# Spreading C over eight heads by DMA instead of by a TensorE product, with the plan of step times made anew

## The chip, the cores and the metric

The kernel runs on one core of a Trainium2 chip. The metric is the device time of one execution in microseconds (us); lower is better. A core has TensorE (PE, matrix products), VectorE (DVE), ScalarE (ACT), GpSimd (POOL) and SyncE (SP, whose queue issues every DMA of this kernel). Each engine runs its own list of instructions in order and waits on semaphores for the others.

## The reference

One layer: x = x + ssm(layernorm(x)), then x = x + ffn(layernorm(x)), on x of 8 x 1024 x 256 in float32. The change lies in the state space part, here cut to what it touches:

```python
z0, x0 = zxbcdt[..., :512], zxbcdt[..., 512:1024]
xBC = silu(causal_conv4(zxbcdt[..., 1536:2080]) + conv_b)
dt = softplus(zxbcdt[..., -8:] + dt_bias)
A = -exp(A_log)                       # 8 heads of 64 channels
x, Bm, Cm = xBC[..., :512], xBC[..., 512:528], xBC[..., 528:544]
def step(h, inp):                     # state h: heads x 64 x 16
    x_t, B_t, C_t, dt_t = inp
    h = exp(dt_t * A) * h + dt_t * x_t * B_t
    return h, einsum('bhpn,bn->bhp', h, C_t) + D_param * x_t
# then layernorm(y), y * sigmoid(y @ W_gate.T), concat with silu(z0) * x0, @ W_out.T
# ffn: gelu(x @ ternary(W_fc).T), layernorm, @ ternary(W_proj)
```

All eight heads share the same 16 rows of C. The part of y that comes from the state carried in is, for each head, the state times C scaled by that head's decay up to the time step; so C is wanted on 8 x 16 = 128 rows, once for each head.

## The kernel before

The 8 x 1024 time steps are cut into 16 blocks of 512 (two a sequence), and each block into four chunks of 128. For every block 16 tasks are made (`ln1, conv, silu, dt_chain, inputs, decay, states, mix, yout, gate, skip, out, turn3, ln3, fc, proj`), each a Python generator that yields a `Need` (an engine, what must be ready, how many PSUM banks, which table of ScalarE's functions) ahead of each step.

The order on the engines is written out at build time by a list scheduler: it keeps the tasks of up to five blocks alive, works out for each when its next step could start by the costs in `Engine.guess` and `Engine.dma`, and of the steps that could start within `EPS` = 0.4 of the earliest it takes the one whose due time is least. The due time is the step's number in `PLAN`, plus `PERIOD` (76.4) times the block, plus the block's entry in `SHIFT`. A step that wants another function table starts later by `SWITCH`. So `PLAN` settles ties between steps that can start together; it holds no step back. A DMA counts as 0.5 on SP there. What comes out is five fixed lists of instructions.

The places that the change touches:

- `silu(i)`: once channel group 4 of the convolution is done (`conv4`), ScalarE writes silu of B into `xbuf[64:80, 4]` and silu of C into `cv[64:80, i % 2, 4]` (token `ct`), 16 rows of 512 each; then it runs over the 512 x channels in two instructions.
- `decay(i)`: TensorE sums the log decays (`pick` with `segL`), ScalarE's Exp writes `ec` (128 x 512: head and state row by time). Then `rep` (16 x 128, ones where the state rows agree) times C gives C on all 128 rows in a PSUM bank (token `rep_mm`), and VectorE multiplies it into `ec` (token `ce`), after copying the chunk ends to `dec`. Then come the scaled B (`BE`) and the product of B and C (`Gm`).
- `states(i)` needs `dec` and `ce`; `yout(i)` multiplies the states with `ec` and adds the products within the chunk, then normalises y.
- The users of SP's queue: `hilo_T`, which splits a matrix into two float16 halves in `hb` and has both transposed by DMA (`xnT` for a block's input, `x3T` ahead of `fc`, `hT` for each of the four chunks of `fc`, ahead of `proj`'s products on the same chunk); `load_x`; the residual's load in `out`; `dt_chain`'s four copies `segR<-segL`; and the output.

The weights are float16 pairs, and a product of two pairs is three matmuls (`three`, the profile's line 166). Products of float32 tiles, `rep`'s among them, are run as they are.

Of the kernel before, what the change touches and what calls it, by code (L numbers as in the profile page):

```python
# [8 lines left out]
P = 128  # L9
T = 512  # L10
# [9 lines left out]
for _n, _w in (("dtb", 1), ("alog", 8), ("dcol", 4), ("lng", 4), ("lnb", 4), ("bg", 4), ("cw", 20), ("cb", 5),  # L20
# [8 lines left out]
PLAN = {  # L29
    "conv": (-101.6, -85.2, -84.1, -81.5, -77.0, -79.4, -67.1, -67.5, -66.0, -61.0, -57.8, -59.7, -55.3, -49.8,  # L30
        -46.5, -45.2, -44.4, -42.1),
    "decay": (-4.9, -4.9, 0.3, 8.1, 8.6, 9.2, 12.6, 17.1, 17.2, 10.0, 19.8),
    "dt_chain": (-66.4, -63.6, -38.0, -33.7, -26.6, -21.4, -21.3, -18.8, -18.1, -17.2),
# [4 lines left out]
    "gate": (108.4, 112.0, 122.6, 122.9, 120.0, 117.1, 125.3, 125.7, 125.1, 130.0, 131.7, 130.6, 130.8, 135.1,  # L38
        136.7, 135.8),
    "inputs": (-21.6, -5.6, 0.7, 1.1, 1.6, 4.8, 2.1, 7.1),  # L40
    "ln1": (-111.6, -95.8, -93.5, -92.7, -93.9, -92.0),
    "ln3": (198.2, 200.0),
    "mix": (4.7, 9.5, 27.4, 29.3, 20.0, 32.8, 27.1, 33.6, 33.9, 37.3, 41.0, 47.1),
    "out": (106.3, 145.0, 162.2, 168.2, 184.7, 197.2, 194.4, 191.4, 195.3),
    "proj": (227.6, 230.4, 229.2, 239.6, 238.3, 242.4, 249.7, 254.7),
    "silu": (-32.6, -33.5, -33.7),
    "skip": (50.6, 53.1, 52.7, 56.2, 117.3, 117.3, 117.8, 115.9, 121.7, 122.1, 120.3, 121.4, 118.2, 99.2,
        100.5, 101.8, 103.4, 128.5, 127.9, 127.2),
    "states": (20.0, 24.7, 26.0),
    "turn3": (195.1, 195.6, 193.9, 199.7),  # L50
    "wffn": (88.0, 97.1, 101.0, 103.0, 108.9, 103.0, 113.3, 113.1, 116.3, 115.9, 118.0),
    "wgate": (70.5,),
    "win": (12.4, 16.7, 23.0),
    "wout": (88.8, 89.0),
    "yout": (29.7, 29.6, 47.0, 75.6, 76.1, 75.3, 74.2, 63.8, 65.9, 65.6, 67.1, 68.6, 70.4, 74.1, 74.8, 82.6,
        84.1, 85.8, 89.1, 89.0, 90.4, 93.6, 94.6, 97.4, 91.5, 101.1, 101.6, 103.5, 102.6, 100.1, 105.7, 102.2,
        104.7, 105.7),
}
PERIOD = 76.4
SHIFT = (0.0, 0.0, 0.0, 0.0, 0.0, 0.0, 0.0, 0.0, 0.0, 0.0, 0.0, 0.0, 0.0, -0.4, 0.0, 2.4)  # L60
AHEAD = 5
EPS = 0.4

# [132 lines left out]
def build(nc, x_d, small_d, const_d, c16_d, lnw_d, win_d, wg_d, wout_d, wfc_d, wpj_d, out_d):  # L196
# [5 lines left out]
    with ctx:  # L202
        def sb(name, shape, dt=f32):
            return ctx.enter_context(nc.sbuf_tensor(name, shape, dt))

        def sem(name):
            return ctx.enter_context(nc.semaphore(name))
# [13 lines left out]

        small = sb("small", [P, NSMALL])
        const = sb("const", [P, 3 * P + 2])
        ident, smask, rep = const[:, 0:P], const[:, P:2 * P], const[64:80, 2 * P:3 * P]
        ul = sb("ul", [P, 2, P], f16)
        upto, after = ul[:, 0, :], ul[:, 1, :]
        ones16 = sb("ones16", [P, P], f16)[:, :]
# [435 lines left out]
        def decay(i):  # L663
            cs, ct, bb = cv[:, i % 2], cv[64:80, i % 2, 4, :], xbuf[64:80, 4, 3:T + 3]
            yield Need(V, ("car", i - 1), ("S", 4 * i) if i % 2 else ("car", i - 1))
            if i % 2 == 0:
                dn["S", 4 * i] = V.do([old("car", i - 1)], "memset", S[:, (4 * i) % 5, :], 0.0)
            yield Need(PE, ("L", i), ("car", i - 1), banks=1, func="Exp")
            b, f = take()
            PE.wait(dn["L", i], f, dn["tk", 0])  # L670
            for c in range(NCH):
                m = PE.do([], "matmul", b[:, chunk(c)], pick[:, c, :, :], segL[:, i % 2, :], start=True, stop=True)
            dn["ec_mm", i] = m
            yield Need(A, ("ec_mm", i), func="Exp")
            dn["ec", i] = A.do([m, old("car", i - 1)], "activation", ec[:, :], b[:, :], ACT.Exp)
            give(b, dn["ec", i])
            yield Need(PE, ("a", i), ("be", i - 1), banks=1, func="Exp")
            b, f = take()
            PE.wait(f, t_ul)
            for q in range(2):  # L680
                m = PE.do([dn["a", i]], "matmul", b[:, 0:32].rearrange("p (c e) -> p c e", c=NCH), after,
                          ahl[:, i % 2, q, :, 3:11], start=(q == 0), stop=(q == 1))
            dn["ahl_read", i] = m
            yield Need(A, ("ahl_read", i), func="Exp")
            dn["es", i] = A.do([m, old("be", i - 1)], "activation", esuf[:, :, :].rearrange("p c e -> p (c e)"),
                               b[:, 0:32], ACT.Exp)
            give(b, dn["es", i])
            yield Need(PE, ("ct", i), ("S_done", i - 1), banks=1)
            b, f = take()
            m = PE.do([dn["ct", i], f, tc], "matmul", b[:, :], rep, ct, start=True, stop=True)  # L690
            dn["rep_mm", i] = m
            yield Need(V, ("rep_mm", i), ("ec", i))
            v = V.do([dn["ec", i], old("S_done", i - 1)], "tensor_copy", dec[:, :],
                     ec[:, :].rearrange("p (c t) -> p c t", c=NCH)[:, :, P - 1])
            dn["ce", i] = V.do([m, v], "tensor_tensor", ec[:, :], b[:, :], ec[:, :], ALU.mult)
            give(b, dn["ce", i])
            yield Need(PE, ("es", i), ("S_done", i - 1), ("L", i), banks=1)
            b, f = take()
            PE.wait(f)
            for c in range(NCH):  # L700
                m = PE.do([dn["ct", i]], "transpose", b[:, 16 * c:16 * c + 16], bb[:, chunk(c)], ident[64:80, 64:80])
            dn["be_mm", i] = m
            yield Need(V, ("be_mm", i))
            dn["be", i] = V.do([m, dn["es", i], old("S_done", i - 1), dn["L", i]], "tensor_tensor", BE[:, :, :, :],
                               b[:, 0:64].rearrange("p (c n) -> p c n", c=NCH).unsqueeze(2).broadcast_to([P, NCH, 8, 16]),
                               esuf[:, :, :].unsqueeze(3).broadcast_to([P, NCH, 8, 16]), ALU.mult)
            give(b, dn["be", i])
            yield Need(PE, ("ct", i), ("EM_all", i - 1), banks=1)
            b, f = take()
            PE.wait(f)  # L710
# [406 lines left out]
```

How the kernel before makes its waits and increments, by code:

```python
    def wait(self, *tokens):  # L87
        for t in tokens:
            if t is None:
                continue
            if isinstance(t, list):
                self.wait(*t)
                continue
            sem, value = t
            self.due = max(self.due, t.when)
            if self.met.get(id(sem), 0) >= value:
                continue
            self.met[id(sem)] = value
            self.queue.append(lambda e, sem=sem, value=value: e.wait_ge(sem, value))
# [33 lines left out]
    def do(self, waits, name, *args, **kw):  # L133
        self.wait(*waits)
        if self.kind == "ACT":
            self.load(args[2].name)
        self.count += 1
        sem = self.sem
        method = {
            "matmul": lambda e: e.matmul(*args, **kw), "transpose": lambda e: e.transpose(*args, **kw),
            "activation": lambda e: e.activation(*args, **kw),
            "tensor_tensor": lambda e: e.tensor_tensor(*args, **kw),
            "tensor_scalar": lambda e: e.tensor_scalar(*args, **kw),
            "scalar_tensor_tensor": lambda e: e.scalar_tensor_tensor(*args, **kw),
            "tensor_copy": lambda e: e.tensor_copy(*args, **kw), "memset": lambda e: e.memset(*args, **kw),
            "bn_stats": lambda e: e.bn_stats(*args, **kw), "bn_aggr": lambda e: e.bn_aggr(*args, **kw),
        }[name]
        self.queue.append(lambda e: method(e).then_inc(sem, 1))
        return Token(sem, self.count, self.spend(name, args, kw))
```

## Time and profile before

| what | value |
|---|---|
| median of 3 runs | 1315.84 us (1315.33 to 2367.39) |
| time of the profiled execution | 1316.03 us |
| its span | 1314.2 us |
| instructions | 22448 |
| PE busy | 1169.8 us, 89% |
| PE loading weights (PEld, overlaps PE) | 740.1 us, 56% |
| DVE busy | 1070.4 us, 81% |
| ACT busy | 937.2 us, 71% |
| POOL busy | 363.7 us, 28% |

The span runs from the first to the last instruction; the 1.8 us beyond it are start and end. The rows in the section further down are of this one execution. Of the three runs two lie within 0.51 us of each other, and the third is an outlier. L140, L141, L142, L144 and so on are the lines of `Engine.do` that issue matmul, activation, tensor_tensor and scalar_tensor_tensor; L178 and L180 are the transposing and the plain DMA; so instructions are told apart by their tiles.

### The profile page before, as it was taken

To read this page: it belongs to the slowest core of one execution; us is meant where nothing else is said; L and a number is where in the kernel's file an instruction comes from. 1 tells how busy PE (TensorE), PEld (TensorE's weight loads), DVE (VectorE), ACT (ScalarE), POOL (GpSimd) and SP (SyncE) were. 2 spreads that over 40 slices of the span, in tenths; PEclk is the share of its full clock that TensorE was granted. 3 is DMA by queue.
4 is the path that set the end of the run, shared out by engine and by line. 5 is a ranking of instruction groups with operands and counts; after the bars stand their busy time and mean duration, and the time that the engine had idled before them with its cause. 6 is when DMAs were issued, how large, how long until landed. Compare 5 with 4: busy or idle time off the path is not lost.

```text
span 1314.2 us, 22448 instructions
## 1 busy us (share of the span) xinstructions
PE 1169.8 (89%) x8566; PEld 740.1 (56%) x8566; DVE 1070.4 (81%) x2116; ACT 937.2 (71%) x1502; POOL 363.7 (28%) x388
## 2 busy tenths in 40 slices
PE   3566889999999999999999998999899999999875
PEld 1344465656566565656566564656656565746453
DVE  6878798888988988888989896888888887766534
ACT  5746377878789696767878776777868686665734
POOL 0010315142422415142330514142050424232320
PEclk9777899999999999999999999999999999999987
DMA  4610102222242323223232313223232231312433
GB/s 142 201 33 1 33 1 63 51 71 61 64 82 65 65 55 74 44 57 82 65 66 65 66 33 89 57 65 80 51 66 58 56 65 49 66 49 49 97 64 80
DMA packets 234874, 84.89 MB, mean 65 GB/s; under 512 B 205712, under 2 KB 233104, under 8 KB 234768
## 3 DMA queue, kind: packets, MB, share of 16 engines
q1 hardware_dynamic: 234768, 83.47, 28.8%
q8 instruction: 68, 1.11, 0.4%
q14 instruction: 38, 0.31, 0.1%
HBM read 24.32 MB, written 8.39 MB: 25 GB/s over the span
## 4 chain that ended last, share of the span: by engine, by line
PE 43%; DVE 28%; ACT 14%; DMA 10%; issue 4%; POOL 1%; DVEq 0%; SPq 0%
PE bank L140 23%; PE bank L166 20%; DMA hT<-hb 8%; DVE hn L144 4%; DVE cv L144 4%; ACT h L141 3%; DVE EM L144 3%; ACT L161 3%; DVE hb L142 3%; DVE tg L144 2%; ACT hb L141 2%; DVE sz L144 2%; DVE S L144 1%; DVE yhl L142 1%; DVE x L143 1%
## 5 line engine op out<-in xcount | busy, mean ns | idle before, releaser
L166 PE MATMUL bank<-xnT,win 128*128 128x512 f16 (+1 forms) x1040 | 267.9, 390 | 17.0 <-DMA xnT<-hb 16.8
L144 DVE SCALAR_TENSOR_TENSOR cv<-xbuf,cws,cv 128x512 f32<-128x512 f32 (+1 forms) x240 | 179.5, 749 | 12.6 <-ACT cv L141 4.8
L140 PE MATMUL bank<-wpj,hT 128*128 128x256 f16 x1040 | 136.3, 289 | 47.9 <-DMA hT<-hb 42.0
L166 PEld LDWEIGHTS bank<-xnT,win 128*128 128x128 f16 (+1 forms) x1040 | 102.2, 102 | 130.1 <-issue 32.7
L166 PE MATMUL bank<-yhl,wg 128*128 128x512 f16 x704 | 165.3, 384 | 3.7 <-DVE yhl L142 3.6
L140 PEld LDWEIGHTS bank<-wpj,hT 128*128 128x128 f16 x1040 | 103.7, 103 | 80.8 <-ACT hb L141 16.7
L161 ACT ACT_TABLE_LOAD x97 | 124.5, 1283 | 15.8 <-DVE dtt L144 7.1
L140 PE MATMUL bank<-wfc,x3T 128*128 128x512 f16 x512 | 128.5, 385 | 4.3 <-DMA x3T<-hb 4.3
L142 POOL TENSOR_TENSOR rsy<-rsy,mhalf 128x1 f32<-128x1 f32 x64 | 59.4, 928 | 241.2 <-DVE rsy L143 228.3
L166 PEld LDWEIGHTS bank<-yhl,wg 128*128 128x128 f16 x704 | 68.5, 99 | 88.8 <-issue 7.8
L142 POOL TENSOR_TENSOR cat<-sz,cat 128x512 f16<-128x512 f32 x64 | 87.0, 1360 | 110.7 <-ACT cat L141 110.7
L141 ACT ACTIVATE h<-bank,rs 128x512 f32<-128x512 f32 x128 | 87.4, 685 | 39.4 <-PE bank L140 37.3
L142 POOL TENSOR_TENSOR rs<-rs,mhalf 128x4 f32<-128x4 f32 x32 | 40.9, 1279 | 258.0 <-DVE rs L143 250.4
L144 DVE SCALAR_TENSOR_TENSOR EM<-EM,Gm 128x512 f32<-128x512 f32 x128 | 100.2, 825 | 8.6 <-ACT EM L141 8.5
L142 POOL TENSOR_TENSOR caty<-tg,caty 128x512 f16<-128x512 f32 x64 | 79.9, 1248 | 86.9 <-ACT caty L141 86.9
L142 POOL TENSOR_TENSOR rsh<-rsh,mhalf 128x1 f32<-128x1 f32 x64 | 36.2, 565 | 233.2 <-DVE rsh L143 233.2
L166 PE MATMUL bank<-wout,cat 128*128 128x256 f16 x768 | 94.4, 273 | 2.2 <-POOL cat L142 1.9
L140 PE MATMUL bank<-const,yT 128*128 128x128 f32 x512 | 79.9, 281 | 14.9 <-DVE yT L144 8.2
L142 DVE TENSOR_TENSOR hb<-hn,hb 128x1024 f16<-128x1024 f32 x64 | 78.1, 1220 | 12.1 <-ACT hb L141 9.0
L166 PE MATMUL bank<-wout,caty 128*128 128x256 f16 x704 | 87.3, 273 | 0.0
L141 ACT ACTIVATE hsq<-h,hmu 128x1024 f16<-128x1024 f32 x64 | 73.3, 1146 | 19.0 <-DVE hmu L143 19.0
L141 ACT ACTIVATE xbuf<-bank 128x512 f32<-128x512 f32 (+1 forms) x80 | 47.2, 590 | 53.5 <-PE bank L140 53.2
(133 smaller groups left out, 2368.2 us busy)
## 6 DMA issues: line engine op xcount, KB each, us to landing
x<-in_x SPq DMA_DIRECT2D x32, 512.0 KB, 4.2
out_y<-x SPq DMA_DIRECT2D x15, 512.0 KB, 2.9
hT<-hb SPq DMA_TRANSPOSE x128, 3.2
segR<-segL SPq DMA_DIRECT2D x64, 6.0 KB
caty<-in_wg SPq DMA_DIRECT2D x1, 1024.0 KB, 5.6
x<-in_wout SPq DMA_DIRECT2D x1, 1024.0 KB, 9.2
hT<-in_wfc SPq DMA_DIRECT2D x1, 1024.0 KB, 11.2
hn<-in_wpj SPq DMA_DIRECT2D x1, 1024.0 KB, 13.5
```

The source lines that it names most:

```text
L140: "matmul": lambda e: e.matmul(*args, **kw), "transpose": lambda e: e.transpose(*args, **kw),
L141: "activation": lambda e: e.activation(*args, **kw),
L142: "tensor_tensor": lambda e: e.tensor_tensor(*args, **kw),
L143: "tensor_scalar": lambda e: e.tensor_scalar(*args, **kw),
L144: "scalar_tensor_tensor": lambda e: e.scalar_tensor_tensor(*args, **kw),
L161: self.queue.append(lambda e: e.preload_act_table_set(name))
L166: self.queue.append(lambda e: e.matmul(*args, **kw))
```

## The change

1. The 16 rows of C are copied eight times, by eight DMAs on SP's queue, from `cv[64:80, i % 2, 4]` to a new SBUF tile `crep` (128 x 512, float32). They are issued in `silu(i)` right after the step that makes C; they wait for `ct` and for the multiplication `ce` of the block before.
2. The product with `rep`, its PSUM bank and its step are gone. VectorE's multiplication reads `crep` where it read the bank, and waits for the eighth copy.
3. `cd_read`, on which the next but one writer of that part of `cv` waits, now includes the copies.
4. `PLAN` and the last two entries of `SHIFT` are made anew. `silu` has a step more and `decay` one less, and other steps' due times move.

The diff, with the plan cut to the entries that move most:

```diff
 PLAN = {
...
-    "decay": (-4.9, -4.9, 0.3, 8.1, 8.6, 9.2, 12.6, 17.1, 17.2, 10.0, 19.8),
-    "dt_chain": (-66.4, -63.6, -38.0, -33.7, -26.6, -21.4, -21.3, -18.8, -18.1, -17.2),
+    "decay": (-23.2, -23.2, -22.1, -10.2, -9.7, -5.7, -1.2, -1.1, -8.3, 1.5),
+    "dt_chain": (-66.4, -63.6, -38.0, -33.7, -26.6, -21.4, -16.6, -18.8, -18.1, -17.2),
...
-    "inputs": (-21.6, -5.6, 0.7, 1.1, 1.6, 4.8, 2.1, 7.1),
-    "ln1": (-111.6, -95.8, -93.5, -92.7, -93.9, -92.0),
-    "ln3": (198.2, 200.0),
-    "mix": (4.7, 9.5, 27.4, 29.3, 20.0, 32.8, 27.1, 33.6, 33.9, 37.3, 41.0, 47.1),
+    "inputs": (-20.7, -4.7, 1.6, 2.0, 2.5, 5.7, 3.0, 8.0),
+    "ln1": (-118.6, -101.1, -98.0, -94.4, -98.4, -95.6),
+    "ln3": (198.2, 196.1),
+    "mix": (5.7, 8.6, 24.4, 28.4, 19.1, 31.9, 26.8, 32.7, 33.0, 36.4, 40.1, 46.2),
...
-    "silu": (-32.6, -33.5, -33.7),
...
+    "silu": (-48.3, -33.2, -33.0, -33.2),
...
-    "states": (20.0, 24.7, 26.0),
+    "states": (17.8, 17.4, 21.8),
...
 PERIOD = 76.4
-SHIFT = (0.0, 0.0, 0.0, 0.0, 0.0, 0.0, 0.0, 0.0, 0.0, 0.0, 0.0, 0.0, 0.0, -0.4, 0.0, 2.4)
+SHIFT = (0.0, 0.0, 0.0, 0.0, 0.0, 0.0, 0.0, 0.0, 0.0, 0.0, 0.0, 0.0, 0.0, -0.4, -2.4, 14.8)
...
+        s_rep = sem("s_rep")
...
-        ident, smask, rep = const[:, 0:P], const[:, P:2 * P], const[64:80, 2 * P:3 * P]
+        ident, smask = const[:, 0:P], const[:, P:2 * P]
...
+        crep = sb("crep", [P, T])
...
             dn["ct", i] = A.do([old("cd_read", i - 2)], "activation", cs[64:80, 4, :], cs[32:48, 4, :], ACT.Silu)
+            yield Need(SP, ("ct", i), ("ce", i - 1))
+            for e in range(8):
+                dn["crep", i] = SP.dma([dn["ct", i], old("ce", i - 1)], s_rep, 16 * (8 * i + e + 1),
+                                       crep[16 * e:16 * e + 16, :], cs[64:80, 4, :])
...
-            yield Need(PE, ("ct", i), ("S_done", i - 1), banks=1)
-            b, f = take()
-            m = PE.do([dn["ct", i], f, tc], "matmul", b[:, :], rep, ct, start=True, stop=True)
-            dn["rep_mm", i] = m
-            yield Need(V, ("rep_mm", i), ("ec", i))
+            yield Need(V, ("crep", i), ("ec", i), ("S_done", i - 1))
             v = V.do([dn["ec", i], old("S_done", i - 1)], "tensor_copy", dec[:, :],
                      ec[:, :].rearrange("p (c t) -> p c t", c=NCH)[:, :, P - 1])
-            dn["ce", i] = V.do([m, v], "tensor_tensor", ec[:, :], b[:, :], ec[:, :], ALU.mult)
-            give(b, dn["ce", i])
+            dn["ce", i] = V.do([dn["crep", i], v], "tensor_tensor", ec[:, :], crep[:, :], ec[:, :], ALU.mult)
...
-            dn["cd_read", i] = m
+            dn["cd_read", i] = [m, dn["crep", i]]
```

The other edits of `PLAN` are of the same kind: `skip` 5.5 earlier, `out` 1.5 to 4.4 earlier, the weights' preparation `wffn` up to 9.7 later (`wout` its second entry 10.3 later), and single entries elsewhere.

## Rows read from the trace of the kernel before

**Rows 1.** The page: busy time, share and instructions of each engine.

```profile
PE 1169.8 (89%) x8566; PEld 740.1 (56%) x8566; DVE 1070.4 (81%) x2116; ACT 937.2 (71%) x1502; POOL 363.7 (28%) x388
```

**Rows 2.** The windows: stretch, length, busy by engine (PE, PEld, DVE, ACT, POOL), clock, DMA.

```profile
600.00:700.00 100.00, 95.24 (x725) 62.73 (x726) 88.88 (x180) 80.01 (x130) 29.75 (x35) 1.00 0.32 64
```

**Rows 3.** The page: the chain that ended last, by engine, by line.

```profile
PE 43%; DVE 28%; ACT 14%; DMA 10%; issue 4%; POOL 1%; DVEq 0%; SPq 0%
PE bank L140 23%; PE bank L166 20%; DMA hT<-hb 8%; DVE hn L144 4%; DVE cv L144 4%; ACT h L141 3%; DVE EM L144 3%; ACT L161 3%; DVE hb L142 3%; DVE tg L144 2%; ACT hb L141 2%; DVE sz L144 2%; DVE S L144 1%; DVE yhl L142 1%; DVE x L143 1%
```

**Rows 4.** The timeline of SP: start, length (eight merged), operation, count.

```profile
226.49 33.31 SPq L178 DMA_TRANSPOSE hT<-hb  x8
...
600.95 33.24 SPq L178 DMA_TRANSPOSE hT<-hb  x8
...
674.84 33.27 SPq L178 DMA_TRANSPOSE hT<-hb  x8
...
1052.05 27.65 SPq L178 DMA_TRANSPOSE hT<-hb  x8
```

**Rows 5.** The groups: the product, VectorE's multiplication, one from SBUF, `proj`'s products.

```profile
L140 PE MATMUL bank<-cv,const 16*128 16x512 f32 x32 | 18.9, 671 | 1.7 <-ACT ec L141 1.7
L142 DVE TENSOR_TENSOR ec<-bank,ec 128x512 f32<-128x512 f32 x16 | 11.1, 691 | 6.2 <-PE bank L140 5.9
L142 DVE TENSOR_TENSOR yhl<-yT,yhl 128x512 f16<-128x512 f32 x64 | 44.4, 694 | 6.7 <-ACT yhl L141 6.5
...
L140 PE MATMUL bank<-wpj,hT 128*128 128x256 f16 x1040 | 136.3, 289 | 47.9 <-DMA hT<-hb 42.0
```

**Rows 6.** The timeline of PE: the product and what follows, two blocks.

```profile
318.54 1.12 PE L140 MATMUL bank<-cv,const 16*128 16x512 f32 x2
319.62 1.91 PE L140 MATMUL bank<-wpj,hT 128*128 128x256 f16 x16
...
618.60 1.12 PE L140 MATMUL bank<-cv,const 16*128 16x512 f32 x2
620.00 1.91 PE L140 MATMUL bank<-wpj,hT 128*128 128x256 f16 x16 [0.28 <-ACT EM L141]
```

**Rows 7.** The timeline: VectorE's split; the page: a transpose's us to landing.

```profile
615.45 1.23 DVE L142 TENSOR_TENSOR hb<-hn,hb 128x1024 f16<-128x1024 f32 x1 [0.39 <-ACT hb L141]
hT<-hb SPq DMA_TRANSPOSE x128, 3.2
```

**Rows 8.** Line 180: SP's ns for one issue, min/median/max; the landing of segR.

```profile
L180 SPq DMA_DIRECT2D segR<-segL x64: 697/698/922, 40.8 to 1119.3; - x64
L180 SPq DMA_DIRECT2D out_y<-x x19: 333/396/583, 264.2 to 1312.1; - x19
DMA to landing us min/median/max: 3.4/3.5/3.6
```

**Rows 9.** The timelines: hT's last transposes, C's silu and what follows.

```profile
615.44 2.61 SPq L178 DMA_TRANSPOSE hT<-hb  x2
...
630.91 3.28 SPq L178 DMA_TRANSPOSE hT<-hb  x2
639.36 0.63 ACT L141 ACTIVATE cv<-cv 16x512 f32<-16x512 f32 x1
641.55 0.38 SPq L180 DMA_DIRECT2D x<-in_x  x1
649.04 2.63 SPq L178 DMA_TRANSPOSE x3T<-hb  x2
```

**Rows 10.** The timelines in block 0: C's silu and the product.

```profile
26.89 0.63 ACT L141 ACTIVATE cv<-cv 16x512 f32<-16x512 f32 x1
47.31 1.12 PE L140 MATMUL bank<-cv,const 16*128 16x512 f32 x2
```

**Rows 11.** The page: the loads of ScalarE's function tables.

```profile
L161 ACT ACT_TABLE_LOAD x97 | 124.5, 1283 | 15.8 <-DVE dtt L144 7.1
```

**Rows 12.** The timeline of PE, near the end: waiting for a transpose.

```profile
1289.15 3.57 PE L140 MATMUL bank<-wpj,hT 128*128 128x256 f16 x16 [6.51 <-DMA hT<-hb]
```

More of the change, by code:

```diff
@@ L37 @@
         245.8, 245.6, 246.3, 247.0, 247.8, 247.1),
-    "gate": (108.4, 112.0, 122.6, 122.9, 120.0, 117.1, 125.3, 125.7, 125.1, 130.0, 131.7, 130.6, 130.8, 135.1,
+    "gate": (108.4, 112.0, 122.6, 122.9, 120.0, 117.1, 125.3, 125.7, 125.1, 130.0, 131.7, 130.6, 130.8, 134.4,
         136.7, 135.8),
-    "inputs": (-21.6, -5.6, 0.7, 1.1, 1.6, 4.8, 2.1, 7.1),
-    "ln1": (-111.6, -95.8, -93.5, -92.7, -93.9, -92.0),
-    "ln3": (198.2, 200.0),
-    "mix": (4.7, 9.5, 27.4, 29.3, 20.0, 32.8, 27.1, 33.6, 33.9, 37.3, 41.0, 47.1),
-    "out": (106.3, 145.0, 162.2, 168.2, 184.7, 197.2, 194.4, 191.4, 195.3),
-    "proj": (227.6, 230.4, 229.2, 239.6, 238.3, 242.4, 249.7, 254.7),
-    "silu": (-32.6, -33.5, -33.7),
-    "skip": (50.6, 53.1, 52.7, 56.2, 117.3, 117.3, 117.8, 115.9, 121.7, 122.1, 120.3, 121.4, 118.2, 99.2,
-        100.5, 101.8, 103.4, 128.5, 127.9, 127.2),
-    "states": (20.0, 24.7, 26.0),
-    "turn3": (195.1, 195.6, 193.9, 199.7),
-    "wffn": (88.0, 97.1, 101.0, 103.0, 108.9, 103.0, 113.3, 113.1, 116.3, 115.9, 118.0),
+    "inputs": (-20.7, -4.7, 1.6, 2.0, 2.5, 5.7, 3.0, 8.0),
+    "ln1": (-118.6, -101.1, -98.0, -94.4, -98.4, -95.6),
+    "ln3": (198.2, 196.1),
+    "mix": (5.7, 8.6, 24.4, 28.4, 19.1, 31.9, 26.8, 32.7, 33.0, 36.4, 40.1, 46.2),
+    "out": (104.6, 143.3, 160.5, 163.8, 183.2, 195.5, 192.7, 189.7, 193.6),
+    "proj": (227.6, 233.3, 232.1, 242.5, 241.2, 242.4, 249.7, 254.7),
+    "silu": (-48.3, -33.2, -33.0, -33.2),
+    "skip": (45.1, 47.6, 47.2, 50.7, 111.8, 111.8, 112.3, 110.4, 116.2, 116.6, 114.8, 115.9, 112.7, 93.7, 95.0,
+        96.3, 97.9, 123.0, 122.4, 121.7),
+    "states": (17.8, 17.4, 21.8),
+    "turn3": (195.1, 195.6, 193.9, 196.2),
+    "wffn": (97.7, 106.8, 110.7, 112.2, 118.6, 112.7, 123.0, 122.8, 117.9, 125.6, 127.0),
     "wgate": (70.5,),
-    "win": (12.4, 16.7, 23.0),
-    "wout": (88.8, 89.0),
+    "win": (12.5, 16.8, 21.9),
+    "wout": (86.0, 99.3),
     "yout": (29.7, 29.6, 47.0, 75.6, 76.1, 75.3, 74.2, 63.8, 65.9, 65.6, 67.1, 68.6, 70.4, 74.1, 74.8, 82.6,
-        84.1, 85.8, 89.1, 89.0, 90.4, 93.6, 94.6, 97.4, 91.5, 101.1, 101.6, 103.5, 102.6, 100.1, 105.7, 102.2,
+        84.1, 85.8, 89.1, 83.9, 90.4, 93.6, 94.6, 97.4, 91.5, 101.1, 101.6, 103.5, 102.6, 100.1, 105.7, 102.2,
         104.7, 105.7),
```

2 rows, old and new, of the table PLAN are left out of this document.

## The prediction

> **What bounds the kernel now.** I read the page's busy shares first, then the windows, then the chain that ended last, then the order on each engine around the product that goes.
>
> The page has TensorE (PE) busy for 89% of the span and VectorE for 81% [rows 1]. The windows show that this is an average over a fill, a steady part and an end: in a steady stretch of 100 us PE is busy 95.2 us at a granted clock of 1.00, the 2.4 GHz level, VectorE 88.9 us, ScalarE 80.0 us [rows 2]. So PE is the fullest engine, but no engine is full, and the chain runs through several: PE 43%, VectorE 28%, ScalarE 14%, DMA 10% [rows 3]. The kernel is a set of fixed lists that wait for each other, with PE closest to its limit.
>
> The starts of `hT`'s transposes give the period. From 600.95 to 674.84 it is 73.9 us. From 226.49 to 1052.05 there are 11 periods [rows 4]; at 73.9 us each they would be 812.9 us, and they take 825.6: 12.7 us lie in periods longer than the regular one. These are a property of the order, and a new plan can lose or keep them.
>
> **What the change removes.** The product with `rep` is two records a block: 32 records, 18.9 us busy [rows 5]. Where the next work follows at once, start to start it is 319.62 - 318.54 = 1.08 us [rows 6]; six more blocks read like that (0.96 to 1.08 us, and 2.0 us for the one in the fill at half clock), some 1.05 us each. The weight loads lie under the products: nothing for them. So TensorE loses 16 x 1.05 = 16.8 us of work.
>
> What of it was on the path? In 8 of the 16 blocks the next group is a product with `hT` that waits 0.28 to 1.33 us after it, as at 620.00 [rows 6]. That wait is for the transpose: VectorE's split runs 615.45 + 1.23 = 616.68, and a transpose takes 3.2 us to land [rows 7], so 619.9. In the old order, taking away the product in these blocks only makes the wait longer, 1.4 us where it was 0.28. Gain there: 0. In the other 8 it is 8 x 1.05 = 8.4 us. The new plan can put other products into the gap; for half of it that is another 8 x 1.05 / 2 = 4.2 us, so 12.6 us. The other estimate goes by the chain: PE's share of it is 43% [rows 3], and 0.43 x 16.8 = 7.2 us. I take about the middle, **10 us**; the ends are 0 (each microsecond given back to a later wait) and 16.8.
>
> **What it adds.** (a) VectorE's multiplication reads SBUF where it read PSUM. It takes 691 ns with one operand in a bank; a tensor_tensor of the same size with both operands in SBUF takes 694 ns [rows 5]. 16 x 3 ns is nothing: 0. It no longer waits for PE (5.9 us of idle time in all 16 [rows 5], a third of a microsecond each); what follows it on VectorE is then ready no sooner, so 0 too.
>
> The Trainium skill ("VectorE: DVE Perf Modes", on the errata of SBUF sources) gives 58 cycles of fixed cost for an operand in SBUF and 120 for one in PSUM. By that rule the 16 multiplications would be 16 x 62 / 0.96 GHz = 1.0 us shorter, an estimate; the rows show no such difference (691 against 694 ns), so the sum stays at 0.
>
> (b) Eight DMAs a block on SP, 128 in all. The trace has no such copy; the nearest, from SBUF to SBUF, is `segR<-segL` with 0.70 us on the queue, and the cheapest plain DMA took 0.33 us [rows 8]. So eight take 2.7 to 5.6 us of SP; I take 5.6, since it is the same kind. In a steady block C's silu ends at 639.36 + 0.63 = 640.0 [rows 9]. The copies would then occupy SP until 645.6. Behind them waits the residual's load, at 641.55, which would go out 4.1 us late; its half of `x2` is for a later block's `out`, so that is hidden. The next that matters is `x3T` at 649.04 [rows 9], 3.4 us after the copies' end. So the cover is that gap in SP, and the cost is 0; if the gap is gone, see the second rival. The engines are busy with DMA for a third of the time [rows 2]; the copies add 4.2 MB to 84.9.
>
> (c) The copies' latency: 5.6 us of issue and 3.5 us from issue to landing [rows 8], 9.1 us in all, where the product took 1.1. The shortest time from C's silu to the product is in block 0: 47.31 - 27.52 = 19.8 us [rows 10]; in a steady block the product comes 618.60 + 73.9 - 640.0 = 52.5 us after it [rows 4, 6, 9]. Hidden everywhere: 0. The wait of the first copy for the last block's multiplication is met long before.
>
> (d) `cd_read` also waits for the copies, but the writer is two blocks on: 0. One PSUM bank less is held for 2 us a block: a small gain inside the 10 us.
>
> **What it moves.** `decay`'s due times are some 18 earlier, C's silu 15.7 earlier, the last block is 14.8 back. The due time only settles ties. `ec` cannot come before the carried products of the block before free its tile, and needs Exp's table, so I expect it where the table is loaded anyway. For the fill, 0. For the end, where PE waits 6.5 us for one transpose [rows 12], block 15 stepping back for block 14 can gain or lose up to the 12.4 us by which it moves; I take 0 and keep the rest for the range.
>
> **The sum.** The profiled execution took 1316.03 us (span 1314.2 and 1.8 around it), 0.2 us over the median of 1315.84. 1316.0 - 10 + 0 + 0 = **1306 us**.
>
> **The rivals.**
>
> *All of it and a smoother order: 1286.* The whole 16.8 us comes back and the irregular periods go: 1316.0 - 16.8 - 12.7 = 1286.5. For it: PE's 95% and the freed bank. Against: new orders bring irregular periods of their own, and 8 blocks wait for a transpose there.
>
> *The copies delay a transpose: 1351, slower.* Place: SP, in a steady block. If C's silu comes 15.7 us earlier, as its due time says, it ends at 624.3, in the middle of `fc`, and the copies lie on SP from 624.3 to 629.9. The third pair of `hT`'s transposes is over at 618.05, the fourth starts at 630.91 [rows 9]. It fits, by 1.0 us. Once the silu ends after 625.3 and before 634.2, the fourth pair goes out late, by 5.6 us at most and 2.8 on average, and PE already waits for these pairs, so it passes on: 16 x 2.8 = 45 us, and 1306 + 45 = 1351. For it: the planner counts 0.5 a copy and not 0.70. Against: it knows of the queue, and the silu would need a table load of its own there.
>
> *Two more table loads a block: 1319.* If the early silu of C or the early `ec` falls between Gelu steps, ScalarE loads a table twice more, 2 x 1.28 us [rows 11] x 16 = 41 us of ScalarE. The loads' share of the chain is 3%, 39 us of their 124.5 [rows 3, 11], so 0.31 x 41 = 13 us is on the path: 1306 + 13 = 1319.
>
> *Nothing comes back: 1316.* If the lists are tied by VectorE, which keeps every instruction and is busy 88.9 us in 100 [rows 2], PE's saving turns into longer waits in all blocks: 1316.0 - 0. For it: eight blocks in which that holds by the rows. Against: PE's 43% of the chain. The Trainium skill ("Perfetto Trace Analysis", Identifying the Most-Contended Engine) says that matmul busy time is a poor measure and the weight loads' share a better one. By that rule PE is at 56% and VectorE, at 81%, is the most contended [rows 1], and the time would stay at 1316; the chain of waits speaks against it, and it is this rival's case.
>
> **Chances.** The forecast 0.48, with 1297 to 1312 as its own range; smoother 0.18; nothing back 0.15; table loads 0.10; transposes late 0.09. The range that leaves out half of the smoother case (0.09) and the late transposes (0.09) is **1286 to 1330**. A change of over 2% is what a measurement of this kernel can surely tell from none: below 1289.5 or over 1342.2. Faster by that: 0.12, from the smoother case and a good end. Slower: 0.07. The same: 0.81.
>
> **What would show it.** The record of `rep` is gone and PE's busy time falls by some 19 us; VectorE's stays within 2 us. The 128 copies take about 0.70 us each on SP and lie between `hT`'s last pair and `x3T`. VectorE never waits for a copy. Table loads stay at 97, give or take four. The steady period is 73.2 to 73.6 us, and PE's waits for `hT`, 42 us now [rows 5], grow by some 5. It is wrong if the period falls by 1 us or more (the product was wholly on the path), if it rises (look at SP before `hT`'s fourth pair, and at the count of table loads), or if the gain lies in the first 226 or the last 120 us, which I put at nothing.

## The result and the profile after

| kernel | median, us | lowest to highest |
|---|---|---|
| before | 1315.74 | 1315.33 to 2367.39 |
| changed | 1304.25 | 1302.24 to 1306.39 |

The ratio of changed to before is 0.9914, with a 95% interval of 0.989 to 0.9938: 11.3 us, and 8 to 14 us by the interval. The forecast was 1306. The execution of the kernel before that took 2367.39 us stands alone and is in no comparison. On the chips of the later experiments executions of one and the same kernel lie up to 16 us apart, so there only medians and intervals are compared, and a trace is read for places and not for its total. Where a difference in us is given beside a ratio it is worked out from the ratio; the difference of the medians can be up to 4 us away from it.

The page of the changed kernel, whose profiled execution took 1306.39 us (span 1304.6), answers to [rows 1], [rows 3] and [rows 11]:

```profile
span 1304.6 us, 22529 instructions
PE 1150.3 (88%) x8534; PEld 732.5 (56%) x8534; DVE 1061.3 (81%) x2116; ACT 929.3 (71%) x1500; POOL 348.3 (27%) x388
...
PE 44%; DVE 23%; ACT 21%; DMA 7%; issue 4%; POOL 1%; SPq 0%; DVEq 0%
...
L140 PE MATMUL bank<-wpj,hT 128*128 128x256 f16 x1040 | 133.2, 285 | 43.6 <-DMA hT<-hb 38.9
...
L161 ACT ACT_TABLE_LOAD x95 | 121.9, 1283 | 13.4 <-PE bank L140 11.7
```

TensorE's busy time fell by 19.5 us, of which the product's records are 18.9. The span fell by 9.6. So in this trace TensorE stands idle 9.9 us longer than before (154.3 against 144.4). The same kernel was traced once more, in the run `f0_after` further down: span 1292.0, TensorE busy 1142.8, idle 149.2. Both are given below where they differ. The next view tells where the time went. It is the timeline of SP, at the starts of `hT`'s transposes, as in [rows 4]: start, length, operation, count; the changed kernel, then one more row of the kernel before.

```profile
216.69 35.46 SPq L178 DMA_TRANSPOSE hT<-hb  x8
...
583.05 34.93 SPq L178 DMA_TRANSPOSE hT<-hb  x8
...
655.17 35.38 SPq L178 DMA_TRANSPOSE hT<-hb  x8
...
877.57 29.29 SPq L178 DMA_TRANSPOSE hT<-hb  x8
```

```profile
902.03 32.58 SPq L178 DMA_TRANSPOSE hT<-hb  x8
```

| stretch | before | changed | difference | changed, second trace |
|---|---|---|---|---|
| start to block 0's first `hT` transpose | 226.5 | 216.7 | -9.8 | 218.2 |
| nine periods from there (before: to 902.03) | 675.5 | 660.9 | -14.6 | 657.0 |
| the rest | 412.2 | 427.0 | +14.8 | 416.8 |
| span | 1314.2 | 1304.6 | -9.6 | 1292.0 |

In this trace the fill and the steady part are 24.4 us shorter, and the end gives 14.8 of that back. In the second trace, of the same lists, the end gives back 4.6: the signs hold, the size of the end does not. Three of the nine periods are 72.1 us (583.05 to 655.17 is one), five are 73.1 to 73.9 and the last is 77.2; before, the regular one was 73.9. I had put 10 us on the steady part and nothing on the other two.

The copies, in the groups by tile (ns min/median/max, first and last start) and in the timeline of SP and ACT in a steady block, beside [rows 8] and [rows 9]:

```profile
L180 SPq DMA_DIRECT2D crep<-cv x128: 527/589/1494, 27.9 to 1059.1; - x128
DMA to landing us min/median/max: 1.9/1.9/2.9
...
628.04 0.63 ACT L141 ACTIVATE cv<-cv 16x512 f32<-16x512 f32 x1
628.69 5.00 SPq L180 DMA_DIRECT2D crep<-cv  x8
630.27 1.05 ACT L141 ACTIVATE hb<-x 128x1024 f16<-128x1024 f32 x1
633.79 2.64 SPq L178 DMA_TRANSPOSE x3T<-hb  x2
```

They go out the moment C is ready, at 628.7, and hold SP for 5.0 us. The first half of `x3T`'s source is ready at 630.27 + 1.05 = 631.3, and its transpose starts at 633.79: the copies hold it up by 2.5 us. This is the mechanism of my slower rival, on another transfer. No product of `fc` waits for it in the steady part.

### The profile page after: what moved, and what is told of

Read it like the earlier page. It is cut to its first block, busy times and chain, and to the rows that moved or that the text cites. A ratio compares the mean times of both kernels' runs of the same rounds, so it can differ in the third digit from the quotient of the medians.

```text
span 1304.6 us, 22529 instructions
## 1 busy us (share of the span) xinstructions
PE 1150.3 (88%) x8534; PEld 732.5 (56%) x8534; DVE 1061.3 (81%) x2116; ACT 929.3 (71%) x1500; POOL 348.3 (27%) x388
## 4 chain that ended last, share of the span: by engine, by line
PE 44%; DVE 23%; ACT 21%; DMA 7%; issue 4%; POOL 1%; SPq 0%; DVEq 0%
PE bank L166 22%; PE bank L140 22%; DMA hT<-hb 6%; DVE cv L144 3%; ACT L161 3%; ACT hb L141 3%; DVE hb L142 3%; DVE hn L144 3%; ACT cv L141 3%; ACT h L141 2%; ACT yT L141 2%; ACT EM L141 2%; ACT yhl L141 2%; DVE tg L144 2%; ACT xbuf L141 2%
## 5 line engine op out<-in xcount | busy, mean ns | idle before, releaser
L166 PE MATMUL bank<-xnT,win 128*128 128x512 f16 (+1 forms) x1040 | 265.1, 386 | 17.1 <-DMA xnT<-hb 16.9
L144 DVE SCALAR_TENSOR_TENSOR cv<-xbuf,cws,cv 128x512 f32<-128x512 f32 (+1 forms) x240 | 182.0, 759 | 10.3 <-ACT cv L141 3.5
L166 PE MATMUL bank<-yhl,wg 128*128 128x512 f16 x704 | 167.9, 388 | 21.6 <-DVE yhl L142 12.7
L140 PE MATMUL bank<-wpj,hT 128*128 128x256 f16 x1040 | 133.2, 285 | 43.6 <-DMA hT<-hb 38.9
L161 ACT ACT_TABLE_LOAD x95 | 121.9, 1283 | 13.4 <-PE bank L140 11.7
L142 POOL TENSOR_TENSOR cat<-sz,cat 128x512 f16<-128x512 f32 x64 | 80.2, 1253 | 160.4 <-ACT cat L141 160.4
L142 POOL TENSOR_TENSOR caty<-tg,caty 128x512 f16<-128x512 f32 x64 | 84.8, 1324 | 97.7 <-ACT caty L141 97.7
L142 POOL TENSOR_TENSOR rsy<-rsy,mhalf 128x1 f32<-128x1 f32 x64 | 51.2, 800 | 222.5 <-DVE rsy L143 172.7
L144 DVE SCALAR_TENSOR_TENSOR EM<-EM,Gm 128x512 f32<-128x512 f32 x128 | 93.5, 772 | 2.1 <-ACT EM L141 1.8
L142 POOL TENSOR_TENSOR rs<-rs,mhalf 128x4 f32<-128x4 f32 x32 | 38.2, 1194 | 208.5 <-DVE rs L143 200.4
L141 ACT ACTIVATE cat<-sz 128x512 f16<-128x512 f32 x64 | 40.1, 627 | 68.2 <-DVE sz L144 51.2
L144 DVE SCALAR_TENSOR_TENSOR tg<-tg,yT 128x512 f32<-128x512 f32 x64 | 58.9, 921 | 33.9 <-ACT tg L141 33.9
```

Of the source, the lines that this page charges most:

```text
L140: "matmul": lambda e: e.matmul(*args, **kw), "transpose": lambda e: e.transpose(*args, **kw),
L141: "activation": lambda e: e.activation(*args, **kw),
L142: "tensor_tensor": lambda e: e.tensor_tensor(*args, **kw),
L144: "scalar_tensor_tensor": lambda e: e.scalar_tensor_tensor(*args, **kw),
L161: self.queue.append(lambda e: e.preload_act_table_set(name))
L166: self.queue.append(lambda e: e.matmul(*args, **kw))
```

## The experiments

Each of the three groups was run beside the kernel before on the same chip; its medians there were 1315.91, 1315.80 and 1316.53. The first and the third group ran on one chip, the second on another.

### The old order kept

Here the planner sees the kernel before, so that the lists of all engines stay word for word the same; the product is taken out of TensorE's list, or doubled, and the copies are put into SP's list, without a cost in the planner. For the product taken out (`phantom` leaves the planner the product's cost and issues no instruction):

```diff
+            keep = (SP.free_at, SP.due, SP.pipe)
+            for e in range(8):
+                dn["crep", i] = SP.dma([dn["ct", i], old("ce", i - 1)], s_rep, 16 * (8 * i + e + 1),
+                                       crep[16 * e:16 * e + 16, :], cs[64:80, 4, :])
+            SP.free_at, SP.due, SP.pipe = keep
...
-            m = PE.do([dn["ct", i], f, tc], "matmul", b[:, :], rep, ct, start=True, stop=True)
+            m = phantom(PE, [dn["ct", i], f, tc], b, rep, ct)
...
-            dn["ce", i] = V.do([m, v], "tensor_tensor", ec[:, :], b[:, :], ec[:, :], ALU.mult)
...
+            t = dn["crep", i]
...
+            dn["ce", i] = V.do([t, v], "tensor_tensor", ec[:, :], crep[:, :], ec[:, :], ALU.mult)
```

**The product out, the copies in.**

> Old plan and old order on every engine, only the product with rep left out and the eight copies of C on SP put in its place, at the moment C is ready; the output is whole. Half of the product on the path (the prediction's count of blocks in the old order): 8 of 16 blocks give back 1.05 us, 8.4 us in all, 1307.4. All on the path: 16.8 us, 1299. Nothing on the path (VectorE ties the lists): 1315.8, within 1 us.

Measured: 1307.9, ratio 0.9938 (0.9902 to 0.9974), so 8.2 us less, where 8.4 was forecast; 16.8 us and 0 are both outside the interval (3.4 to 12.9 us). The timeline of TensorE in three blocks shows where it comes back and where not; the first is the block at 318.54 in [rows 6], the third the one at 618.60 (lines are four higher in this kernel):

```profile
315.74 1.91 PE L144 MATMUL bank<-wpj,hT 128*128 128x256 f16 x16 [1.36 <-ACT EM L145]
...
462.01 0.22 PE L144 MATMUL bank<-ahl,ul 128*128 128x32 f16 x2
463.56 1.91 PE L144 MATMUL bank<-wpj,hT 128*128 128x256 f16 x16 [1.33 <-ACT EM L145]
...
609.90 0.22 PE L144 MATMUL bank<-ahl,ul 128*128 128x32 f16 x2
611.51 1.91 PE L144 MATMUL bank<-wpj,hT 128*128 128x256 f16 x16 [1.40 <-DMA hT<-hb]
```

Where the product stood is now a wait of 1.33 to 1.40 us, where behind the product it was mostly 0.28 to 0.36: the 1.1 us went into the wait, as the prediction said (1.4 us). In some blocks the wait ends with ScalarE's `EM`, which gives back the bank that `proj` takes, and in others with the transpose. But it is so in more blocks than the eight counted. The block at 318.54, which had no wait and was counted as a whole 1.05 us, waits 1.36 us now; in block 12 the next group waits 0.63 us, where there was no wait, and in block 10 a `proj` group twelve matmuls on waits 0.86 us, where it waited 0.26. That leaves five whole blocks (0, 1, 2, 14 and 15) and parts of two, 5 to 6 us by the same count.

**The copies added, the product kept.** They stand at the same place on SP, and nothing reads them.

```diff
+            for e in range(8):
+                dn["crep", i] = SP.dma(...)
```

> Old plan, old order, product kept and used; the eight copies are added on SP and read by nobody. Copies hidden: within 1 us of 1315.8. Copies late for a transpose or in the way of one: up to 16 x 2.8 = 45 us more, and PE's waits for hT grow from 42 us.

Measured: 1315.6, ratio 0.9996 (0.9968 to 1.0024). The copies cost nothing that can be measured, and by the interval at most some 3 us.

**The copies in block 0 alone, the product out.** The later blocks multiply by block 0's C, so the output is not the reference's.

```diff
+            if i == 0:
+                ...
+            else:
+                dn["crep", i] = dn["crep", 0]
```

> As the first, but the copies are made in block 0 alone, and all later blocks multiply by block 0's C (so the state's part of y is wrong from block 1 on; the work of VectorE is the same). If the copies cost nothing it equals the first within 1 us; if the copies take part of the product's gain, it is faster than the first by that part.

Measured: 1312.6, ratio 0.9973 (0.9945 to 1.0002). It is not faster than the first, so the copies take nothing from the gain. It should have equalled the first within 1 us and its median is 4.7 us over it; the intervals overlap. The two have the same lists but for SP, so I take them as two measurements of one thing: 3.6 and 8.2 us back, by these two runs a fifth to a half of the product's 16.8 us, and some 5 us with the two ratios weighted by their executions.

The traces agree with the smaller part. But for the product and the copies, the lists of all engines are the same up to about 950 us in these kernels and in the old kernel with other last shifts (`g4_before_shift`, below), so their places can be compared:

| trace | product | first `hT` transpose | nine periods | start of the tenth |
|---|---|---|---|---|
| before | in | 226.5 | 675.5 | 902.0 |
| `e2_dma` | in | 227.4 | 672.0 | 899.4 |
| `g4_before_shift` | in | 225.5 | 671.7 | 897.1 |
| `e1_out` | out | 222.6 | 669.7 | 892.3 |
| `e3_no_copies` | out | 225.4 | 671.7 | 897.1 |

The mean of the two without it is 4.8 us ahead of the mean of the three with it, and single traces differ as much. A regular period is 73.9 us with the product and without it (666.33 to 740.29 in `e1_out`): in the steady blocks nothing came back. The prediction took the irregular periods for a property of the order. The longest of the trace before (78.7 us) isn't one. In the old kernel with other last shifts, with the same lists at this place, it is 74.3 us; first the trace before, then that one:

```profile
522.29 36.46 SPq L178 DMA_TRANSPOSE hT<-hb  x8
...
600.95 33.24 SPq L178 DMA_TRANSPOSE hT<-hb  x8
```

```profile
521.66 33.57 SPq L178 DMA_TRANSPOSE hT<-hb  x8
...
595.99 33.25 SPq L178 DMA_TRANSPOSE hT<-hb  x8
```

Over the first 30 us of that block (539 to 569) the granted clock is 0.89 in the first and 1.00 in the second.

**The product twice.**

```diff
+            PE.wait(dn["ct", i], f, tc)
+            PE.queue.append(lambda e, b=b, ct=ct: e.matmul(b[:, :], rep, ct, start=True, stop=True))
             m = PE.do([dn["ct", i], f, tc], "matmul", b[:, :], rep, ct, start=True, stop=True)
```

> Old plan and order, the product with rep run twice in each block (16.8 us more of TensorE's work, same result). If half of such a product is on the path because 8 blocks wait for a transpose right behind it, only the wait's 0.28 to 1.33 us (4 us in all) can hide it: 12.8 us more, 1328.6. If nothing is on the path: 1315.8. If all: 1332.6.

Measured: 1329.3, ratio 1.0084 (1.0055 to 1.0112): 11.1 us more (7.2 to 14.7), and 13.4 by the medians, for 12.8 forecast. Again neither 0 nor 16.8. Adding costs more than removing gives back (5 us): the wait behind the product is short (0.3 us), so most of a second product passes it, while without the first one the next thing to wait for is there at once. A price found by doubling isn't the gain of removing.

### Mechanism and plan apart

**The changed kernel again.**

> The changed kernel itself again, beside the others of this call: 1304, 0.991 of the kernel before.

Measured: 1307.2, ratio 0.9909 (0.9874 to 0.9944).

**The new mechanism with the old plan.** The planner makes its order freely, with the copies in it; all other entries and SHIFT are as in the kernel before.

```diff
-    "decay": (-23.2, -23.2, -22.1, -10.2, -9.7, -5.7, -1.2, -1.1, -8.3, 1.5),
+    "decay": (-4.9, -4.9, 0.3, 8.1, 8.6, 12.6, 17.1, 17.2, 10.0, 19.8),
-    "silu": (-48.3, -33.2, -33.0, -33.2),
+    "silu": (-32.6, -32.6, -33.5, -33.7),
...
```

> The changed kernel with the old plan and the old shifts (the copies' step due with C's silu at -32.6, the product's entry dropped); the planner makes its order freely with the copies in it. If the product's removal alone is the gain and the plan adds nothing, it equals the kept order, 1307 to 1308. If the new plan gives the other half of the product back, it is 4 to 8 us slower than the changed kernel, 1308 to 1312. If the new plan costs at the end what the steady part gained, it is faster than the changed kernel, 1297 to 1302.

Measured: 1391.7, ratio 1.0577 (1.0553 to 1.06): 76 us slower than before, and 84 us slower than `e1_out`, the same work in the old order. None of the three theories had that. The timeline of TensorE in a regular period (81.8 us, where it was 73.9), then the windows around its longest wait (columns as in [rows 2]), then SP's copies of that period:

```profile
672.14 3.57 PE L140 MATMUL bank<-wpj,hT 128*128 128x256 f16 x16 [5.55 <-DMA hT<-hb]
...
665.00:670.00 5.00, 1.58 (x36) 1.15 (x36) 4.44 (x8) 4.86 (x9) 0.55 (x1) 0.88 0.39 75
670.00:675.00 5.00, 2.86 (x14) 2.03 (x15) 2.80 (x6) 3.22 (x5) 0.00 (x0) 0.50 0.18 35
...
676.26 0.39 SPq L180 DMA_DIRECT2D out_y<-x  x1
676.70 5.26 SPq L180 DMA_DIRECT2D crep<-cv  x8
```

TensorE comes to the fourth `proj` group with nothing else ahead of it and waits 5.55 us for its transpose; after that idle time the granted clock is 0.50, the 1.2 GHz level, and the sixteen matmuls take 3.57 us where at full clock they take 1.91. The copies come after all this, at 676.7, so they are not what is late. It is the order, which the planner makes from the due times: in its trace eight of the nine periods are 80 to 84 us and the other is 77. That the old due times don't suit a task with a step more and a step less is my reading; which of the entries tips it wasn't tried. The order also has 116 table loads of 1.28 us where the old one has 97, and what part of the loss they are wasn't tried either.

**The old mechanism with the new plan.** All other entries and SHIFT are as in the changed kernel.

```diff
-    "decay": (-4.9, -4.9, 0.3, 8.1, 8.6, 9.2, 12.6, 17.1, 17.2, 10.0, 19.8),
+    "decay": (-23.2, -23.2, -22.1, -10.2, -9.7, -6.0, -5.7, -1.2, -1.1, -8.3, 1.5),
-    "silu": (-32.6, -33.5, -33.7),
+    "silu": (-48.3, -33.0, -33.2),
...
```

> The kernel before (product on TensorE, no copies) with the new plan and the new shifts (silu's entry for the copies dropped, an entry of -6.0 put in for the product). If the plan is good by itself it is at or below 1315.8; if half of the product is on the path it is 8.4 us over the changed kernel, 1313; if all of it is, 16.8 us over, 1321.

Measured: 1339.1, ratio 1.0173 (1.0136 to 1.021), 23 us slower than before and 32 us slower than the changed kernel. This run has the new shifts too, which by themselves cost the old plan 27 us (the last run below), so it doesn't tell what the plan alone does. In its trace the nine periods are 682.2 us, 7 to 11 more than in the old order, and the rest is 438.2 us, where before it was 412.2; it has 111 table loads. So each mechanism was slower with the other's plan, and the planner's two kernels say little on the price of a product: that needs a kept order.

**The changed kernel with the old last shifts.**

```diff
-SHIFT = (..., -0.4, -2.4, 14.8)
+SHIFT = (..., -0.4, 0.0, 2.4)
```

> The changed kernel with the last two shifts as before (0.0 and 2.4 for -2.4 and 14.8). TensorE's idle time up to 900 us is the same in both traces (99.3 and 96.9 us), after 900 us it is 12 us more in the changed kernel (45 and 57 us). If the shifts of the last two blocks make that, this is up to 12 us faster than the changed kernel, 1292 to 1297. If the end is worse for what stands before it in the order (the new due times of all blocks), it equals the changed kernel, within 2 us, or is slower, since the shifts were chosen for this plan.

Measured: 1295.0, ratio 0.9847 (0.9815 to 0.9879). It is 12.2 us faster than the changed kernel by the medians, 8 by the ratios, whose intervals just touch, and 20.1 us faster than before by the ratios. So the shifts cost the changed kernel some 8 to 12 us. The traces don't show it as the loss at the end: the rest behind the nine periods is 422.1 us here, between the 416.8 and the 427.0 of the changed kernel's two, and 10 more than before. That this part of the order is longer with either pair of shifts stays unexplained.

### The product in the new order, and which shift

**The product put back in the new order.**

```diff
             PE.wait(f, t_ul)
+            keep = PE.due
+            PE.wait(dn["ct", i], tc)
+            PE.due = keep
+            PE.queue.append(lambda e, b=b, ct=ct: e.matmul(b[:, :], rep, ct, start=True, stop=True))
             for q in range(2):
```

> The changed kernel in its own order on every engine, with the product of rep and C run again in each block, just ahead of the product that makes the suffix decays, into the same bank, its result overwritten; everything else as it is. If the new order has put the product's whole time on the path (the plan gave back the other half), this costs 16.8 us: 1304 + 17 = 1321. If half of it is still covered by waits, as in the old order: 1313. If nothing is on the path: 1304.

Measured: 1308.7, ratio 0.9926 (0.9905 to 0.9948), against 0.9914 and 0.9909 of the changed kernel: 1.6 to 2.2 us for 16.8 us of work, and with these intervals not told from 0. All of it on the path would be a ratio of 1.004, and half of it 0.997; both are outside. Nothing reads the product's result here, so this is the price of TensorE's time alone. The timeline of TensorE in one block, the changed kernel ahead and this one behind (the product has a line of its own, L689):

```profile
602.98 0.22 PE L140 MATMUL bank<-ahl,ul 128*128 128x32 f16 x2
603.37 1.91 PE L140 MATMUL bank<-wpj,hT 128*128 128x256 f16 x16 [0.17 <-DVE sty L146]
```

```profile
607.08 1.12 PE L689 MATMUL bank<-cv,const 16*128 16x512 f32 x2
608.13 0.22 PE L140 MATMUL bank<-ahl,ul 128*128 128x32 f16 x2
608.19 1.91 PE L140 MATMUL bank<-wpj,hT 128*128 128x256 f16 x16
```

The product fills the wait, and what it delays beyond that is mostly caught by waits further on. Nine periods are 663.1 us here (216.62 to 879.69), 660.9 and 657.0 in the changed kernel's two traces, and 662.5 and 661.3 in the two with block 14's shift at 0.0: 0.6 to 6.1 us less, for nine products of 1.05. With the product in, the old order takes 671.7 to 675.5 for them, so it is the new order that made the steady part shorter. So my theory that the new plan puts the product's whole time on the path, and gives it back, falls.

**Block 14's shift as changed, block 15's as before; and the reverse.**

```diff
-SHIFT = (..., -0.4, -2.4, 14.8)
+SHIFT = (..., -0.4, -2.4, 2.4)      # and (..., -0.4, 0.0, 14.8)
```

> The changed kernel with block 15's shift as before (2.4) and block 14's as changed (-2.4). If block 15's step back of 12.4 made the loss at the end, this is as fast as with both old shifts, 1295; if block 14's made it, it stays at 1304 to 1307.

> The changed kernel with block 14's shift as before (0.0) and block 15's as changed (14.8). The counterpart: 1304 to 1307 if block 15's step back made the loss, 1295 if block 14's did.

Measured: 1316.2, ratio 0.9996 (0.9976 to 1.0016), and 1296.5, ratio 0.9838 (0.9818 to 0.9858). The first interval is apart from those of the other three, the second from both of the changed kernel's. I had thought that block 15's step back of 12.4 made the loss; it is block 14's step of 2.4 ahead. By the ratios it costs 19.6 us with 2.4 for block 15 (0.9996 against 0.9847) and 9 us with 14.8 (0.9909 against 0.9838). The 14.8 costs nothing alone and mends rather more than half of what -2.4 does. The windows from 900 to 1200 of the four, in the order 0.0/2.4, 0.0/14.8, -2.4/14.8, -2.4/2.4 (columns as in [rows 2]):

```profile
900.00:1200.00 300.00, 278.32 (x2105) 181.16 (x2103) 234.10 (x458) 211.47 (x346) 86.94 (x97) 0.97 0.29 59
```

```profile
900.00:1200.00 300.00, 277.94 (x2103) 181.36 (x2102) 230.73 (x452) 214.63 (x348) 87.37 (x94) 0.97 0.28 59
```

```profile
900.00:1200.00 300.00, 273.27 (x2068) 174.86 (x2066) 227.67 (x436) 213.64 (x340) 84.04 (x89) 0.97 0.27 56
```

```profile
900.00:1200.00 300.00, 267.02 (x2019) 170.62 (x2017) 219.19 (x426) 203.33 (x323) 77.50 (x86) 0.97 0.27 55
```

At the same clock TensorE stands idle 21.7, 22.1, 26.7 and 33.0 us in these 300 us, which is the order of the four medians. Up to 900 us the four agree within 1.7 us of busy time. The second trace of -2.4/14.8 has 29.7 us there and is yet the shortest of the five by its span (1292.0), so the count shows where the orders part and not what it costs. In the two with -2.4 TensorE waits longer for VectorE's results, 13.5 and 14.1 us where it is 9.4 and 9.6 with 0.0; that is most of what the third has more, and less than half of what the fourth has, which also waits more for transposes. The longest of these waits in the changed kernel's timeline:

```profile
998.67 1.55 PE L140 MATMUL bank<-EM,Xd 128*64 128x128 f32 x12 [2.86 <-DVE EM L144]
...
1072.29 4.01 PE L166 MATMUL bank<-yhl,wg 128*128 128x512 f16 x11 [2.51 <-DVE yhl L142]
...
1139.13 4.85 PE L166 MATMUL bank<-yhl,wg 128*128 128x512 f16 x11 [3.98 <-DVE yhl L142]
```

That blocks 13 and 14 then ask for VectorE at the same time is my reading; it wasn't tried by itself. The four orders also differ in their table loads, 88, 93, 95 and 97; what part the loads have in it stands untested.

**The old kernel with the new shifts.**

```diff
-SHIFT = (..., -0.4, 0.0, 2.4)
+SHIFT = (..., -0.4, -2.4, 14.8)
```

> The kernel before, product and old plan, with the changed kernel's last two shifts (-2.4 and 14.8). If a block 15 put back is bad whatever the plan, it is some 10 us slower than the kernel before, 1326. If that loss belongs to the new plan's order alone: 1315.8, within 3 us.

Measured: 1345.7, ratio 1.0207 (1.0187 to 1.0227), 27 us slower, more than the 10 that I had expected. The shifts hurt in both plans (here with 103 table loads for 97). With the old shifts, or with 0.0 and 14.8, the change is a gain of 20 to 21 us over before and of some 8 to 9 us over the changed kernel as given.

## Why the prediction was right, and where not

- **The forecast, 1306 for 1304.25.** The sum of -10 us met the measured -11.5, but by other parts: -9.8 and -14.6 us in the fill and the steady part, +14.8 at the end. The nearness is luck in good part: in the second trace the same three are -8.3, -18.5 and +4.6. The steps one by one:
- **The product's size, 16.8 us.** Right: busy time fell by 19.5 us for the 18.9 of its records, and put back in the new order it takes 1.05 us from start to start.
- **Half of it on the path in the old order, 8.4 us.** Right in mechanism, and too large. The waits of 1.33 to 1.40 us came as forecast (1.4), and a second product cost 11.1 for 12.8. But I took the eight blocks without a wait behind the product as paying in full. That nothing waits now doesn't say that nothing will: in one of them the bank and the transpose were ready less than the product's length ahead, and the 1.05 us became a wait too. The runs gave 8.2 and 3.6 us, some 5 together, and five blocks instead of eight. The chain's share of 43% gave 7.2 us, no better and no worse.
- **4.2 us more from filling the gap.** The size of a gain by the new order was underrated and its cause was wrong. With the old shifts and the product in neither, the new order is 12 to 17 us better than the old one (0.9847 against 0.9938 and 0.9973), while the product itself is worth only 1.6 to 2.2 us in it. The shorter periods come from the order, not from the product's time. What in the order makes them shorter no run shows. This is the smoother case in part: I gave it 0.18 and tied it to the removal of the product's whole time, and of its 12.7 us of irregular periods at least 4 were the one execution's and not the order's.
- **The fill at 0.** Wrong by 9.8 and 8.3 us in the two traces. With the old order the first `hT` transpose is at 225.5 to 227.4 us with the product and at 222.6 and 225.4 without it, so most of this is the new order's.
- **The end at 0, up to 12.4 either way.** The step named the right place, and left it out of the sum. It was 14.8 and 4.6 us in the two traces, and by the times of the experiments the shifts cost 8 to 12 us; the part of them that I pointed at, block 15's, was harmless.
- **The copies.** Issue 0.59 us each (0.70 taken), landing 1.9 us (3.5 taken), 5.0 us on SP (5.6 taken), cost 0 (0.9996). Right, with both sizes on the safe side. The gap of 3.4 us ahead of `x3T` was not left: the new order has `x3T` 2.5 us behind the copies, and it is covered further on: in the steady part no product with `x3T` waits.
- **VectorE's multiplication.** 692 ns from `crep` with the order kept, where it was 691 from the bank [rows 5]. (In the changed kernel fifteen take 693 ns, and one, beside GpSimd, 1641.) So the cost is 0, as the rows said, and the 62 cycles by which the Trainium skill ("VectorE: DVE Perf Modes", on the errata of SBUF sources) has an operand in SBUF cheaper than one in PSUM don't show here.
- **What was to be seen.** Table loads 95, within four of 97. VectorE never waits for a copy, as said. Its busy time fell by 9.1 us, not within 2 (the last section says where). The regular period was to be 73.2 to 73.6 us and is 72.1 to 73.9. Of my signs of being wrong two came: three periods fell by 1.8 us, though not because the product was on the path, and 8 to 10 us of the gain lie in the fill. TensorE's waits for `hT` fell from 42.0 to 38.9 us and didn't grow by 5: in the new order other groups fill them. In the kept order they grew from 42.0 to 43.7 us, and the idle time ahead of all `proj` products from 47.9 to 58.0.
- **The rivals.** "Nothing comes back" is true of the regular periods in the old order (73.9 us both ways), and of the whole it is out for the first run's interval and just not for the third's. Its reason fails: with TensorE at 56% by its weight loads, the share that the Trainium skill ("Perfetto Trace Analysis", Identifying the Most-Contended Engine) prefers to the matmuls', a second product still cost 11.1 of 16.8 us. "Table loads" is out by their count. "Transposes late" happened to `x3T`, at no cost.

The first account of the gain, that it is TensorE's time given back, holds for a small part, in the old order alone. Of the 11.5 us of the changed kernel, with the steps taken in this sequence: the product out of the old order -8.2, the new order -12.0, the shifts +8.2 (ratios 0.9938, 0.9847, 0.9909); by the third run it is -3.6, -16.6 and +8.2. In the other sequence (the new order with the product in it is already at 0.9926) the same product is worth 2 us. The parts don't add up to prices of their own.

## What to carry to other kernels

In a kernel of fixed lists, read what stands right behind the instruction that you want to remove, in every repetition: where it waits for something else, the removal only lengthens that wait. Where it doesn't wait, ask how long ahead its inputs were ready: less than the instruction's length, and a wait appears there too. The count of the places left bounds the gain. A planner's due times fit one set of steps; to price a mechanism, keep the order and take out or add the one instruction, since a free order moved the time by 76 us here and the mechanism by 4 to 8. Look at a changed plan's last blocks by themselves: two numbers there took back 8 to 12 us of 20. And before a long period is called a property of the order, look at a second trace of the same lists.

## What the runs showed of the hardware

- A copy from 16 rows of 2 KB in SBUF to 16 other rows took 0.59 us on SP's queue and landed 1.9 us after its issue, where `segR<-segL`, with 3 rows on the receiving side, took 0.70 and 3.5 us [rows 8]. Eight of them in a row beside the float16 transposes left the time as it was.
- VectorE's instructions on two SBUF tensors (`tg`, `EM`) are slow while GpSimd runs one of its own. In the changed kernel's timeline the same instruction takes 1.76 us beside GpSimd's and 0.68 us alone, and GpSimd's own go from 1.16 to 1.67 us:

```profile
640.25 2.59 POOL L142 TENSOR_TENSOR x<-x,r 128x512 f32<-128x512 f32 x2
641.63 1.76 DVE L144 SCALAR_TENSOR_TENSOR tg<-tg,yT 128x512 f32<-128x512 f32 x1
644.13 1.67 POOL L142 TENSOR_TENSOR caty<-tg,caty 128x512 f16<-128x512 f32 x1 [1.29 <-ACT caty L141]
645.87 0.68 DVE L144 SCALAR_TENSOR_TENSOR tg<-tg,yT 128x512 f32<-128x512 f32 x1
647.29 1.16 POOL L142 TENSOR_TENSOR caty<-tg,caty 128x512 f16<-128x512 f32 x1 [1.49 <-ACT caty L141]
```

  Most of the 9.1 us by which VectorE's busy time fell with no instruction less is of this kind: its 128 `EM` products take 93.5 us in the changed kernel, 772 ns each, where they took 100.2 us before, 825 each. No fewer of them meet a 512 wide instruction of GpSimd (27, before 24), but for less of their time: those take 1.10 us in the mean, before 1.44, and all others 0.69 at most.
- Executions of one kernel on one chip differed by up to 16 us (1307.39 to 1323.57 for the kernel before), and the shorter ones have the higher mean granted clock: the changed kernel's at 1293.82 and 1299.47 have 0.968 and 0.967, its four at 1306.83 to 1308.40 have 0.959 to 0.962. Which of the two causes the other isn't shown. A wait of 5.55 us was followed by a stretch at the 1.2 GHz level, in which a group of matmuls took 3.57 us for 1.91; and a wait of 0.3 us was not.
